# A fused attention block on 8 cores: a later and shared buffer for the first Q weights, and a thinner, later filler between the attention matmuls

## The chip, the cores and the metric

The kernel runs on the 8 cores of one Trainium2 chip, each core with one batch element and no traffic between cores. The metric is the device time of one execution in microseconds, which is that of the slowest core. Below, TensorE is called PE, VectorE DVE, ScalarE ACT, GpSimd POOL and SyncE SP, as in the profile.

## What is computed

Per core, x is 2048 x 1024 in f16; there are 16 heads of 64.

```python
xn = _layernorm(x, axis=-1)
q = shape_heads((xn @ wq.T + bq) * scaling);  k = shape_heads(xn @ wk.T + bk);  v = shape_heads(xn @ wv.T + bv)
scores = jnp.einsum('bhtd,bhsd->bhts', q, k)            # causal mask added
attn = jax.nn.softmax(scores.astype(jnp.float32) + mask, axis=-1).astype(jnp.float16)
out = jnp.einsum('bhts,bhsd->bhtd', attn, v)
s = out.transpose(0, 2, 1, 3).reshape(B, T, E) @ wo.T + bo
g = _silu(xn @ weight.T + pooled(xn) @ disha)
x = x + s * g
```

## The kernel before

The program is written by hand as five streams, one for each engine (`S.emit(queue, function, waits, semaphore)`), and each engine executes its stream strictly in the order in which the Python loops emitted it. Nothing reorders it later, so where a line stands in a loop decides what it is queued behind. SP issues nearly all loads, and a wait in its stream holds back every load behind it.

**Stage 1, lines 168 to 316.** For 16 tiles of 128 rows, `a_load` (L201) brings x into one of eight buffers `xin` on SP, `a_stats` and `a_sqrt_f` make mean and 1/std on DVE with a square root on ACT, `a_apply_f` (L234) normalises on DVE, `a_transp` (L242) transposes on PE, and `a_copy` (L251) moves the result to `xnT` on ACT. The loop `for t in range(NTT + 3)` emits statistics of tile t, the normalisation of tile t-1, and the transpose of tile t-2. In it stand, on SP, loads of the feed-forward weights into `wbig` (`mk_wT`, L264), the first half of the Q weights (`emit_wdma(0)` at t == 2, into a buffer `qsb` of its own) and, at t == 12, two loads into `D2`, whose memory is that of `xin0` and `xin1`. After the loop DVE makes eight tiles of `Weff` (L270) from `wbig` and `D2`.

**Stage 2, lines 318 to 413.** Q, K, V and gate products, each a group of 8 matmuls of 512 columns into one PSUM bank: L352 for Q and K, L380 for V, L404 for the gate with its SiLU on ACT (L410). Weights come in halves of 1 MB into `wsb0` and `wsb1`; `emit_wdma(idx)` for idx 0 to 5 names the half, and each waits until the matmuls that read the buffer before are done. `wsb0` shares memory with `xin2` and `xin3`, so whatever is loaded into it has to wait for `a_apply[11]`, the normalisation of tile 11.

**Stage 3, lines 426 to 722.** Attention proceeds by four blocks of 512 queries (tc 0 to 3), in each by 8 pairs of heads (p), in each by 4, 8, 12 or 16 key tiles (sc). One (tc, p, sc) is called a unit; there are 320, numbered u. A unit has two score matmuls (L659, L663, one for each head of the pair, 64 rows each, of N columns: 512, or 512, 384, 256 and 128 in the last four units of a pair, at the diagonal), an exponential on ACT over both (L672), in diagonal units a mask on POOL (L681), and two value matmuls (L698, L702), here called PV, which are emitted about five units later from the list `pvq`. The scores of unit u need the exponential of unit u-2, since two PSUM pairs alternate. After the last PV of a pair, `d_epilogue` copies the two accumulators out on DVE (L585, L587), and the first PV of the next pair waits for that; four small DMAs on SP follow. After the eighth pair the row sums of the block are in `L16`, and two units later DVE takes their reciprocal (L621).

**The filler.** Normalisation and output projection of a finished block are put between the attention matmuls of the next block. `fillq` has for each block 8 N tiles (one matmul L472 each, whose result multiplies `AttnOT` on DVE, L481; the first needs the reciprocal) and 8 E tiles (eight matmuls L515 with `woT` and one L520 with the bias; DVE multiplies and adds, POOL sends the output). `pop_chunk()` emits one N tile, or the next two matmuls of an E tile, so a block has 8 + 8 x 5 = 48 chunks. Each unit adds to `FS["credit"]`, up to `CCAP`, and chunks are popped while the credit is at least `CHUNK` = 440. The core of the loop in the order before:

```python
                    if len(pvq) >= 5:
                        pvq.pop(0)()
                    while FS["credit"] >= CHUNK:
                        ...
                    S.emit("tensor", ...)          # scores of unit u, then its exponential
                    pvq.append(pv_e)
                    FS["credit"] = min(CCAP, FS["credit"] + (300.0 + 2 * N) / 1.2 - 3 * N / 2.4)
```

What is left in `pvq` and `fillq` after the last unit, which includes all 48 chunks of the fourth block, is emitted at the end.

Of the kernel before, what the change touches and what calls it, by code (L numbers as in the profile page):

```python
# [7 lines left out]
F16 = mybir.dt.float16  # L8
# [4 lines left out]
NP = 128  # L13
# [31 lines left out]
def build_program(debug=False):  # L45
# [62 lines left out]
    qsb = at("qsb", [NP, ECH, 512], F16, o_KT + 4096)  # L108
# [42 lines left out]
    with ExitStack() as ctx:  # L151
# [122 lines left out]
        def emit_wdma(idx):  # L274
            src3 = wsrc[idx].rearrange("(ec p) o -> p ec o", p=NP)
            half = idx % 2
            dst = wsb[idx % 2]
            if idx == 0:
                ww = []
                dst = qsb  # L280
            elif idx == 1:
                ww = [("sPE", p_tp[NTT - 1])]
            elif idx == 2:
                ww = [("sPE", p_wdone[0]), ("sDVE", a_apply[11])]
            else:
                ww = [("sPE", p_wdone[idx - 2])]
            c_w[idx] = dma("sync", dst[:], src3[:, :, half * 512:(half + 1) * 512],
                           waits=ww, sem=f"sW{idx % 2}")

        for t in range(NTT + 3):  # L290
# [13 lines left out]
            if t == 2:  # L304
                emit_wdma(0)
            if t == 12:
                dma("sync", D2[0:64, :], disha_d,
                    waits=[("sDVE", a_apply[9])], sem="sD2")
                c_d2b[0] = dma("sync", D2[64:128, :], disha_d, sem="sD2")

# [28 lines left out]
        for pi, (widx0, bias, scale) in enumerate([(0, bqcs, s125), (2, bkcs, None)]):  # L339
            dst = QT if pi == 0 else KT  # L340
            for half in range(2):
# [3 lines left out]
                for tc4 in range(4):  # L345
                    for ocl in range(4):
                        oc = half * 4 + ocl
                        mms = []
                        wt_src = qsb if widx == 0 else wsb[wpar]
                        for ec in range(ECH):  # L350
                            mms.append(lambda g, ps, first, last, w=wt_src, ec_=ec, o_=ocl, t_=tc4:
                                       g.matmul(ps, w[:, ec_, o_ * NP:(o_ + 1) * NP],  # L352
# [6 lines left out]
                        if pi == 1 and half == 0:  # L359
                            ew.append(("sDVE", v_weff[ECH - 1]))  # L360
                            ew.append(("sPE", p_wdone[0]))
# [87 lines left out]
        CCAP = 1500.0  # L449
# [179 lines left out]
        for tc in range(NTC):  # L629
# [5 lines left out]
            for p in range(NPAIR):  # L635
                for sc in range(nsc):
# [4 lines left out]
                    if len(pvq) >= 5:  # L641
                        pvq.pop(0)()
                    while FS["credit"] >= CHUNK:
                        if not pop_chunk():
                            break
                        FS["credit"] -= CHUNK
# [39 lines left out]
                    def mk_pv(p_=p, tb_=tb, sl_=slot, o=off, n=N, a_exp_=a_exp, v_tri_=v_tri,  # L686
                              vv_=v_vevac[sc], s_=sc,
                              first=(sc == 0), last=(sc == nsc - 1)):
                        def go():
# [17 lines left out]
                            if last:  # L707
                                d_epilogue(p_, tb_, pv)
                        return go
                    pv_e = mk_pv()  # L710
                    pvq.append(pv_e)
                    u += 1
                    FS["credit"] = min(CCAP, FS["credit"]
                                       + (300.0 + 2 * N) / 1.2 - 3 * N / 2.4)
# [103 lines left out]
```

How the kernel before makes its waits and increments, by code:

```python
def build_program(debug=False):  # L45
# [669 lines left out]
        while pvq:  # L715
            pvq.pop(0)()
            while lnq:
                lnq.pop(0)[1]()
        while fillq or FS["cur"] is not None:
            assert pop_chunk(), "filler not ready at drain"
        flush_pend()
        flush_pend()
        for i2 in range(2):
            S.emit("gpsimd", lambda g, i_=i2: g.wait_ge(sems[f"sO{i_}"], last_out[i_]))
        if debug:
            dma("sync", dbg["dbg_AOT"], AttnOT[:],
                waits=[("sDVE", tc_norm[3][0]), ("sSH0", sh_last[0])], sem="sDBG")
            gw = [(s, max((v for s2, v in g_done.values() if s2 == s), default=None))
                  for s in ("sACT", "sDVE")]
            dma("sync", dbg["dbg_g"], g_sb[:], waits=gw, sem="sDBG")
            S.emit("sync", lambda g: g.wait_ge(sems["sDBG"], S.cnt["sDBG"]))
        globals()["_last_cnt"] = dict(S.cnt)
        def run(eng, q):
            lastw = {}
            for fn, waits, inc, amt, _val in S.ops[q]:
                for (s, v) in waits:
                    if lastw.get(s, -1) >= v:
                        continue
                    eng.wait_ge(sems[s], v)
                    lastw[s] = v
                inst = fn(eng)
                if inc is not None:
                    inst.then_inc(sems[inc], amt)
```

## Time and profile before

| | us |
|---|---|
| median of 2 runs | 789.04 (788.67 to 789.41) |
| the profiled execution | 790.79 |
| span of its slowest core, core 7, first to last instruction | 789.3 |
| spans of the other cores | 778.7 to 788.7 |
| core 7, mean granted TensorE clock | 0.890 |
| PE busy, ACT busy, DVE busy on core 7 | 653.7, 343.6, 251.5 |

The median is the number that a comparison is made with. The profiled execution took 1.75 us more than the median, 1.5 us of it outside the span of core 7. Busy time of PE includes overlapping matmuls and the half clock, so it is no measure of PE at its peak. A granted clock of 1.00 is 2.4 GHz and 0.50 is 1.2 GHz; a figure between them is a mean over a stretch that had both.

### The profile page before, as it was taken

To read this page: it belongs to the slowest core of one execution; us is meant where nothing else is said; L and a number is where in the kernel's file an instruction comes from. 1 tells how busy PE (TensorE), PEld (TensorE's weight loads), DVE (VectorE), ACT (ScalarE), POOL (GpSimd) and SP (SyncE) were. 2 spreads that over 40 slices of the span, in tenths; PEclk is the share of its full clock that TensorE was granted. 3 is DMA by queue.
4 is the path that set the end of the run, shared out by engine and by line. 5 is a ranking of instruction groups with operands and counts; after the bars stand their busy time and mean duration, and the time that the engine had idled before them with its cause. 6 is when DMAs were issued, how large, how long until landed. Compare 5 with 4: busy or idle time off the path is not lost.

```text
span 789.3 us, 8786 instructions; the slowest of 8 cores (778.7 to 789.3 us)
## 1 busy us (share of the span) xinstructions
PE 653.7 (83%) x2784; PEld 238.5 (30%) x2784; DVE 251.5 (32%) x372; ACT 343.6 (44%) x387; POOL 103.4 (13%) x164
## 2 busy tenths in 40 slices
PE   0457999999999997776888869988769999888665
PEld 0344444444333443221222212322211332222111
DVE  4886544443333000223233242231113222000154
ACT  0322000000000434553567746788864778888500
POOL 0000000000000001441133301321210122121101
PEclk9999999999999999555699967998975999999869
DMA  6424111011000001200211120110010111000022
GB/s 198 140 69 126 36 53 54 1 54 54 0 1 1 0 1 44 84 22 14 61 53 42 55 60 8 51 57 28 9 45 21 35 47 47 8 7 8 14 66 94
DMA packets 25696, 34.86 MB, mean 44 GB/s; under 512 B 4898, under 2 KB 19362, under 8 KB 25652
## 3 DMA queue, kind: packets, MB, share of 16 engines
q1 hardware_dynamic: 23092, 25.91, 11.5%
q0 software_dynamic: 2560, 8.39, 2.8%
q8 instruction: 24, 0.39, 0.2%
q14 instruction: 20, 0.16, 0.1%
HBM read 21.63 MB, written 8.39 MB: 38 GB/s over the span
## 4 chain that ended last, share of the span: by engine, by line
PE 68%; DVE 15%; issue 5%; DMA 4%; ACT 4%; SPq 2%; DVEq 1%; POOL 0%; ACTq 0%; POOLq 0%
PE PS L352 13%; PE PS L698 12%; PE PS L659 11%; PE PS L702 8%; PE PS L380 7%; PE PS L404 7%; PE Q L515 6%; ACT PT L672 4%; DVE OddB L587 3%; DVE OddA L585 3%; DVE L L621 2%; PE Q L472 2%; DMA xin<-x 1%; DVE xn L234 1%; PE PS L383 1%
## 5 line engine op out<-in xcount | busy, mean ns | idle before, releaser
L672 ACT ACTIVATE PT<-PS,neg 128x1024 f16<-128x1024 f32 (+1 forms) x320 | 302.7, 988 | 128.3 <-PE PS L663 125.7
L681 POOL TENSOR_TENSOR PT<-PT,tri 128x256 f16<-128x256 f16 x128 | 86.0, 682 | 611.9 <-ACT PT L672 610.1
L698 PE MATMUL PS<-PT,Vp 128*65 128x512 f16 (+1 forms) x320 | 134.2, 419 | 37.2 <-DVE OddB L587 36.9
L659 PE MATMUL PS<-QT,KT 64*128 64x512 f16 (+1 forms) x320 | 126.1, 395 | 14.1 <-ACT PT L672 10.9
L702 PE MATMUL PS<-PT,Vp 128*65 128x512 f16 (+1 forms) x320 | 127.7, 399 | 0.0
L663 PE MATMUL PS<-QT,KT 64*128 64x512 f16 (+1 forms) x320 | 127.2, 398 | 0.0
L585 DVE CAST OddA<-PS 65x512 f16<-65x512 f32 x32 | 22.0, 687 | 271.4 <-PE PS L702 258.9
L352 PE MATMUL PS<-xnT,wsb 128*128 128x512 f16 x384 | 83.0, 379 | 0.0
L410 ACT ACT_TABLE_LOAD x1 | 1.3, 1283 | 183.2 <-PE PS L404 183.2
L515 PE MATMUL Q<-woT,AttnOT 128*128 128x512 f16 x256 | 76.9, 400 | 4.1 <-DVE AttnOT L481 3.9
L659 PEld LDWEIGHTS PS<-QT,KT 64*128 64x128 f16 x320 | 30.1, 94 | 152.4 <-issue 152.4
L698 PEld LDWEIGHTS PS<-PT,Vp 128*65 128x65 f16 x320 | 36.4, 114 | 114.0 <-issue 108.9
L242 PE MATMUL PS<-eye,xn 128*128 128x128 f32 x128 | 31.0, 424 | 40.9 <-ACT xnT L251 26.6
L380 PE MATMUL PS<-wsb,xnT 128*128 128x512 f16 x256 | 60.8, 380 | 0.0
L404 PE MATMUL PS<-Weff,xnT 128*128 128x512 f16 x256 | 55.4, 379 | 0.0
L352 PEld LDWEIGHTS PS<-xnT,wsb 128*128 128x128 f16 x384 | 37.6, 98 | 45.3
L530 DVE TENSOR_TENSOR esb<-Q,g 128x512 f32<-128x512 f32 x32 | 22.1, 691 | 86.1 <-PE Q L520 47.7
L472 PE MATMUL Q<-L,hsel 16*128 16x512 f16 x32 | 18.1, 598 | 29.4 <-DVE L L621 25.7
L702 PEld LDWEIGHTS PS<-PT,Vp 128*65 128x65 f16 x320 | 39.4, 123 | 0.2
L242 PEld LDWEIGHTS PS<-eye,xn 128*128 128x128 f32 x128 | 25.1, 224 | 46.4 <-issue 46.4
L392 DVE CAST Vp<-PS 128x512 f16<-128x512 f32 x32 | 22.2, 694 | 46.4 <-PE PS L383 46.4
L515 PEld LDWEIGHTS Q<-woT,AttnOT 128*128 128x128 f16 x256 | 24.8, 101 | 31.8 <-issue 12.0
(41 smaller groups left out, 398.4 us busy)
## 6 DMA issues: line engine op xcount, KB each, us to landing
out<-esb POOLq DMA_DIRECT2D x32, 256.0 KB, 2.4
xin<-x SPq DMA_DIRECT2D x16, 256.0 KB, 5.0
wbig<-wT SPq DMA_DIRECT2D x8, 512.0 KB, 7.4
QT<-x SPq DMA_DIRECT2D x32, 128.0 KB, 2.4
wsb<-wkT SPq DMA_DIRECT2D x2, 1024.0 KB, 5.6
wsb<-wvT SPq DMA_DIRECT2D x2, 1024.0 KB, 5.4
woT<-woT SPq DMA_DIRECT2D x1, 2048.0 KB, 9.7
AttnOT<-OddA SPq DMA_DIRECT2D x32, 64.0 KB, 1.9
```

Of the source, the lines that this page charges most:

```text
L242: p_tp[tt] = S.emit("tensor", lambda g, jj=j, p=tt % 2: g.transpose(PS6[:, 4 + jj // 4, (jj % 4) * NP:(jj % 4 + 1) * NP], xn_sb[p][:, jj * ...
L352: g.matmul(ps, w[:, ec_, o_ * NP:(o_ + 1) * NP], xnT[:, ec_, t_ * 512:(t_ + 1) * 512], start=first, stop=last))
L380: g.matmul(ps, xnT[:, ec_, t_ * NP:(t_ + 1) * NP], wsb[w][:, ec_, :], start=first, stop=last))
L404: g.matmul(ps, xnT[:, ec_, t_ * NP:(t_ + 1) * NP], Weff[:, ec_, h * 512:(h + 1) * 512], start=first, stop=last))
L515: S.emit("tensor", lambda g: g.matmul(psF[sl], AttnOT[:, pc_, t_ * NP:(t_ + 1) * NP], woT[:, pc_, o * 512:(o + 1) * 512], start=first, sto ...
L585: evA = S.emit("vector", lambda g: g.tensor_copy(OddA[0:65, :], PS6[0:65, 4, :]), waits=wr, inc="sDVE")
L659: g.matmul(PS6[:, 2 * par_ + 0, o:o + n], KT[0:64, p_, sb2:sb2 + NP], QT[0:64, p_, t + o:t + 512], start=True, stop=True),
L663: g.matmul(PS6[:, 2 * par_ + 1, o:o + n], KT[64:128, p_, sb2:sb2 + NP], QT[64:128, p_, t + o:t + 512], start=True, stop=True),
L672: g.activation(PT[sl_][:, :, o:o + n], PS6[:, 2 * par_:2 * par_ + 2, o:o + n], AF.Exp, bias=neg2[:]), waits=we, inc="sACT")
L681: g.tensor_tensor(PT[sl_][:, :, o:o + NP], PT[sl_][:, :, o:o + NP], t, ALU.mult),
L698: S.emit("tensor", lambda g: g.matmul(psO(0, 65, 0, o, o + n), Vp[:, s_, (2 * p_) * 65:(2 * p_) * 65 + 65], PT[sl_][:, 0, o:o + n], start= ...
L702: pv = S.emit("tensor", lambda g: g.matmul(psO(0, 65, 1, o, o + n), Vp[:, s_, (2 * p_ + 1) * 65:(2 * p_ + 1) * 65 + 65], PT[sl_][:, 1, o:o ...
```

## The change

The change has three parts. `qsb` goes: the first half of the Q weights is loaded into `wsb0`, at t == 12 behind the `D2` loads, with a wait for the normalisation of tile 11; the waits that protected `qsb` go too. In the attention loop the scores of unit u are emitted first, then PV of the oldest unit, then the filler. And the credit for a unit is (172 + 2N)/1.2 - 3N/2.4 in place of (300 + 2N)/1.2 - 3N/2.4, with a cap of 2600 in place of 1500. For N = 512 the credit falls from 463.3 to 356.7, against 440 for a chunk.

```diff
@@ emit_wdma, and where it is called @@
-            dst = wsb[idx % 2]
             if idx == 0:
-                ww = []
-                dst = qsb
+                ww = [("sDVE", a_apply[11])]
             elif idx == 1:
                 ww = [("sPE", p_tp[NTT - 1])]
-            elif idx == 2:
-                ww = [("sPE", p_wdone[0]), ("sDVE", a_apply[11])]
             else:
                 ww = [("sPE", p_wdone[idx - 2])]
...
-            if t == 2:
-                emit_wdma(0)
             if t == 12:
                 dma("sync", D2[0:64, :], disha_d,
                     waits=[("sDVE", a_apply[9])], sem="sD2")
                 c_d2b[0] = dma("sync", D2[64:128, :], disha_d, sem="sD2")
+                emit_wdma(0)
@@ the waits of the projections @@
-                        if pi == 1 and half == 0:
-                            ew.append(("sDVE", v_weff[ECH - 1]))
-                            ew.append(("sPE", p_wdone[0]))
@@ the attention loop @@
-        CCAP = 1500.0
+        CCAP = 2600.0
...
-                    if len(pvq) >= 5:
-                        pvq.pop(0)()
-                    while FS["credit"] >= CHUNK:
-                        if not pop_chunk():
-                            break
-                        FS["credit"] -= CHUNK
                     par = u % 2
...
                     pv_e = mk_pv()
+                    if len(pvq) >= 5:
+                        pvq.pop(0)()
                     pvq.append(pv_e)
                     u += 1
                     FS["credit"] = min(CCAP, FS["credit"]
-                                       + (300.0 + 2 * N) / 1.2 - 3 * N / 2.4)
+                                       + (172.0 + 2 * N) / 1.2 - 3 * N / 2.4)
+                    while FS["credit"] >= CHUNK:
+                        if not pop_chunk():
+                            break
+                        FS["credit"] -= CHUNK
```

The SP stream in the second half of stage 1, before (`xin5` to `xin7` are the loads of tiles 13 to 15; `wsb1` gets the second half of the Q weights):

```order
L166 DMA xin3_67<-x 128x1024
L166 DMA xin4_68<-x 128x1024
L166 DMA D2_72<-disha 64x1024 x2
L166 DMA xin5_69<-x 128x1024
L166 DMA xin6_70<-x 128x1024
L166 DMA xin7_71<-x 128x1024
L166 DMA hsel_109<-hsel 16x1024
L264 DMA wbig_73<-wT 128x1024 x4
L166 DMA wsb1_54<-wqT 128x8x512
```

And the same place of the changed program:

```order
L165 DMA xin3_67<-x 128x1024
L165 DMA xin4_68<-x 128x1024
L165 DMA D2_72<-disha 64x1024 x2
L165 DMA wsb0_53<-wqT 128x8x512
L165 DMA xin5_69<-x 128x1024
L165 DMA xin6_70<-x 128x1024
L165 DMA xin7_71<-x 128x1024
L165 DMA hsel_108<-hsel 16x1024
L263 DMA wbig_73<-wT 128x1024 x4
L165 DMA wsb1_54<-wqT 128x8x512
```

The 1 MB load of Q weights now stands ahead of the x loads of tiles 13 to 15, with its wait for tile 11.

The PE stream in the second block (tc 1) at the first N tiles, before; `PT_63` is unit 31, the last of block 0:

```order
L698 MATMUL PS<-PT_63,Vp 65x128
L702 MATMUL PS<-PT_63,Vp 65x128
L659 MATMUL PS<-QT,KT 128x512
L663 MATMUL PS<-QT,KT 128x512
L698 MATMUL PS<-PT_111,Vp 65x512
L702 MATMUL PS<-PT_111,Vp 65x512
L659 MATMUL PS<-QT,KT 128x384
L663 MATMUL PS<-QT,KT 128x384
L698 MATMUL PS<-PT_112,Vp 65x512
L702 MATMUL PS<-PT_112,Vp 65x512
L472 MATMUL Q<-L_57,hsel 128x512 x3
L659 MATMUL PS<-QT,KT 128x256
```

And in the changed program (the names of `PT` have moved by one number):

```order
L682 MATMUL PS<-PT_63,Vp 65x128
L686 MATMUL PS<-PT_63,Vp 65x128
L643 MATMUL PS<-QT,KT 128x384
L647 MATMUL PS<-QT,KT 128x384
L682 MATMUL PS<-PT_110,Vp 65x512
L686 MATMUL PS<-PT_110,Vp 65x512
L643 MATMUL PS<-QT,KT 128x256
L647 MATMUL PS<-QT,KT 128x256
L682 MATMUL PS<-PT_111,Vp 65x512
L686 MATMUL PS<-PT_111,Vp 65x512
L462 MATMUL Q<-L_57,hsel 128x512 x5
L643 MATMUL PS<-QT,KT 128x128
```

Two scores and two PVs stand between the last PV of the block and the first N tile in both. The scores are one unit further on now, and five N tiles follow one another in place of three.

The PE stream at the end of the fifth pair of block 1, before: the chunk behind the PV of 384 columns, then the last two PVs of the pair, of 256 and 128 columns, each with its chunk:

```order
L515 MATMUL Q<-woT,AttnOT 128x512 x2
L659 MATMUL PS<-QT,KT 128x512
L663 MATMUL PS<-QT,KT 128x512
L698 MATMUL PS<-PT_60,Vp 65x256
L702 MATMUL PS<-PT_60,Vp 65x256
L520 MATMUL Q<-bo_sb,ones_77 128x512
L659 MATMUL PS<-QT,KT 128x512
L663 MATMUL PS<-QT,KT 128x512
L698 MATMUL PS<-PT_61,Vp 65x128
L702 MATMUL PS<-PT_61,Vp 65x128
L515 MATMUL Q<-woT,AttnOT 128x512 x2
```

And in the changed program, from the PV of 384 columns on:

```order
L682 MATMUL PS<-PT_112,Vp 65x384
L686 MATMUL PS<-PT_112,Vp 65x384
L643 MATMUL PS<-QT,KT 128x512
L647 MATMUL PS<-QT,KT 128x512
L682 MATMUL PS<-PT_60,Vp 65x256
L686 MATMUL PS<-PT_60,Vp 65x256
L505 MATMUL Q<-woT,AttnOT 128x512 x2
L643 MATMUL PS<-QT,KT 128x512
L647 MATMUL PS<-QT,KT 128x512
L682 MATMUL PS<-PT_61,Vp 65x128
L686 MATMUL PS<-PT_61,Vp 65x128
L510 MATMUL Q<-bo_sb,ones_76 128x512
```

Behind the PV of 384 columns stand scores now, and no chunk.

## Rows read from the trace of the kernel before

**Rows 1.** Page, granted clock in tenths, 40 equal slices, core 7

```profile
PEclk9999999999999999555699967998975999999869
```

**Rows 2.** Timeline, tiles 1 and 3 of stage 1: start us, duration us, engine, line, what

```profile
7.13 0.43 SPq L166 DMA_DIRECT2D qsb<-wqT  x1
...
18.82 0.69 DVE L209 BATCH_NORM_STATS2 st<-xin 128x6 f32<-128x512 f16 x1 [1.02 <-DMA xin<-x]
```

**Rows 3.** Timeline, the D2 loads, loads of tiles 13 to 15, tiles 11 and 13

```profile
46.12 1.19 SPq L166 DMA_DIRECT2D D<-disha  x2
...
47.37 1.51 SPq L166 DMA_DIRECT2D xin<-x  x3
...
52.07 0.81 DVE L234 TENSOR_SCALAR xn<-xin,mv,rstd 128x1024 f32<-128x1024 f16 x1
...
52.98 0.69 DVE L209 BATCH_NORM_STATS2 st<-xin 128x6 f32<-128x512 f16 x1
```

**Rows 4.** Page part 6, DMA issues: KB each, median us from issue to landing

```profile
xin<-x SPq DMA_DIRECT2D x16, 256.0 KB, 5.0
...
wsb<-wkT SPq DMA_DIRECT2D x2, 1024.0 KB, 5.6
...
wsb<-wqT SPq DMA_DIRECT2D x1, 1024.0 KB, 9.8
```

**Rows 5.** The tile xin, all its loads

```profile
DMA to landing us min/median/max: 2.5/5.0/12.2
```

**Rows 6.** Windows: us, busy PE, PEld, DVE, ACT, POOL, granted clock, DMA share, GB/s

```profile
50.00:52.00 2.00, 1.83 (x8) 1.43 (x8) 1.54 (x5) 0.00 (x0) 0.00 (x0) 1.00 0.92 250
```

**Rows 7.** The chain that ended last, from stage 1 into stage 2

```profile
66.65 1.24 DVE Weff L270
...
81.81 103.76 PE PS L352 x480
```

**Rows 8.** Timeline of PE in block 3 among E chunks

```profile
623.70 0.39 PE L659 MATMUL PS<-QT,KT 64*128 64x512 f16 x1
...
625.00 0.39 PE L659 MATMUL PS<-QT,KT 64*128 64x512 f16 x1
```

**Rows 9.** Timeline of PE in block 3 without filler

```profile
679.01 0.38 PE L698 MATMUL PS<-PT,Vp 128*65 128x512 f16 x1 [1.16 <-DVE OddB L587]
...
679.54 0.49 PE L659 MATMUL PS<-QT,KT 64*128 64x512 f16 x1
...
683.61 0.39 PE L659 MATMUL PS<-QT,KT 64*128 64x512 f16 x1
...
686.47 0.37 PE L659 MATMUL PS<-QT,KT 64*128 64x512 f16 x1
...
687.48 0.37 PE L659 MATMUL PS<-QT,KT 64*128 64x512 f16 x1
...
691.00 0.39 PE L659 MATMUL PS<-QT,KT 64*128 64x512 f16 x1
...
691.87 0.39 PE L659 MATMUL PS<-QT,KT 64*128 64x512 f16 x1
```

**Rows 10.** Windows: block 1 past its filler, block 3 without filler

```profile
434.00:444.50 10.50, 9.00 (x48) 2.92 (x47) 3.28 (x5) 8.32 (x10) 3.96 (x6) 1.00 0.21 71
...
666.10:679.60 13.50, 11.34 (x56) 3.38 (x54) 1.37 (x2) 12.82 (x14) 2.58 (x4) 1.00 0.00 0
679.70:683.10 3.40, 3.40 (x11) 0.66 (x10) 0.00 (x0) 2.23 (x2) 0.00 (x0) 0.50 0.16 39
```

**Rows 11.** Timeline of PE and DVE in block 1 at the first N tiles

```profile
368.30 1.01 PE L472 MATMUL Q<-L,hsel 16*128 16x512 f16 x2 [5.57 <-DVE L L621]
369.12 2.27 DVE L481 TENSOR_TENSOR AttnOT<-AttnOT,Q 128x512 f16<-128x512 f16 x3 [1.08 <-PE Q L472]
...
375.07 0.60 PE L472 MATMUL Q<-L,hsel 16*128 16x512 f16 x1
375.61 0.60 PE L659 MATMUL PS<-QT,KT 64*128 64x512 f16 x1
```

More of the change, by code:

```diff
@@ L107, in build_program @@
     wbig = at("wbig", [NP, 4, E], F32, o_KT + 16384)
-    qsb = at("qsb", [NP, ECH, 512], F16, o_KT + 4096)
     mo = o_misc
@@ L276, in emit_wdma @@
             half = idx % 2
-            dst = wsb[idx % 2]
             if idx == 0:
-                ww = []
-                dst = qsb
+                ww = [("sDVE", a_apply[11])]
             elif idx == 1:
                 ww = [("sPE", p_tp[NTT - 1])]
-            elif idx == 2:
-                ww = [("sPE", p_wdone[0]), ("sDVE", a_apply[11])]
             else:
                 ww = [("sPE", p_wdone[idx - 2])]
-            c_w[idx] = dma("sync", dst[:], src3[:, :, half * 512:(half + 1) * 512],
+            c_w[idx] = dma("sync", wsb[idx % 2][:], src3[:, :, half * 512:(half + 1) * 512],
                            waits=ww, sem=f"sW{idx % 2}")
@@ L348, in build_program @@
                         mms = []
-                        wt_src = qsb if widx == 0 else wsb[wpar]
                         for ec in range(ECH):
-                            mms.append(lambda g, ps, first, last, w=wt_src, ec_=ec, o_=ocl, t_=tc4:
-                                       g.matmul(ps, w[:, ec_, o_ * NP:(o_ + 1) * NP],
+                            mms.append(lambda g, ps, first, last, w=wpar, ec_=ec, o_=ocl, t_=tc4:
+                                       g.matmul(ps, wsb[w][:, ec_, o_ * NP:(o_ + 1) * NP],
                                                 xnT[:, ec_, t_ * 512:(t_ + 1) * 512],
```

## The prediction

> **What bounds the kernel now.** I read the page first for its clock line, then the chain that ended last, then the timeline of each place that the diff touches. The chain goes through DVE in stage 1: the normalisations, then `Weff` from 66.65 us on, and from 81.81 us PE alone, 480 matmuls of L352 in 103.76 us or 216 ns each [rows 7]. So stage 1 is bound by DVE, the projections by PE, and a delay of DVE in stage 1 goes to the end undiminished, since PE's first evacuation in stage 2 stands behind `Weff` on DVE. The clock line is at 9 throughout the projections, and at 5 to 8 in many slices from slice 16 on, which is attention [rows 1].
>
> Attention has two regimes at the full clock, read from the distance between the scores of successive units. Among E chunks PE sets the pace: 623.70 to 625.00 is 1.30 us for scores, two PVs and two L515 [rows 8]. Without filler ACT does: 686.47 to 687.48 is 1.01 us, one exponential of 1024 columns. Right behind a stall or the short diagonal units, when ACT has fallen behind or has had little to do, PE runs free at 691.00 to 691.87, 0.87 us [rows 9]. So a chunk costs PE 1.30 - 0.87 = 0.43 us, but added to a unit that waits for ACT it costs only 0.29.
>
> Once for each pair of heads PE waits for the copies of the accumulators, 1.16 us at 679.01 [rows 9]. In block 3 without filler the clock then falls: 679.70 to 683.10 is at 0.50, behind 13.5 us at 1.00 [rows 10]. The three units from 679.54 to 683.61 take 4.07 us [rows 9] where 0.87 + 0.87 + 1.01 = 2.75 would do, so one such fall costs 1.3 us there. Among chunks, where PE never waits for ACT, 3.4 us at half the clock do 1.7 us of work, so a fall costs up to 1.7.
>
> **Part 1, the Q weights.** What is removed: the 1 MB load at 7.13 us, ahead of the x load of tile 3. The statistics of tile 3 wait 1.02 us for that load [rows 2], and 1 MB takes about 4 us at the 250 GB/s of [rows 6], so without it the tile is there in time: -1.0 us, since DVE is the chain. Later loads in this part never keep DVE waiting, so nothing more is gained.
>
> What is added: SP waits for the normalisation of tile 11, which ends at 52.07 + 0.81 = 52.88, and then issues the 1 MB load and only after it the x loads of tiles 13, 14 and 15. Before, these were issued at 47.37, right behind the D2 loads [rows 3], and were there when the statistics of tile 13 started at 52.98. Queued behind SP's wait are also `hsel` and the four `wbig` loads; they were issued behind `Weff` anyway and shift with it. DVE waits from 52.98 until tile 13 lands, and everything on DVE behind it waits too: the normalisation of tile 12, the transposes, `Weff`, the first Q evacuation. A 1 MB load lands 5.6 us after its issue when it is alone, 9.8 when `wbig` loads stand ahead of it [rows 4]. Here it is nearly alone, the D2 loads of 6.8 us earlier being done, so 5.6. The 256 KB of tile 13 behind it add 1.0 us at 250 GB/s [rows 6]. That makes 52.9 + 5.6 + 1.0 = 59.5 against 52.98: **+6.5 us**. The bound below is the shortest landing of an x load, 2.5 us [rows 5], if its pieces overtook the weights; the bound above is 9.8 + 1.0 - 0.1 = 10.7. I take 6.5, because the row of a lone 1 MB load is nearest. Tiles 14 and 15 land 1 us apart, and one tile takes DVE at least 0.81 + 2 x 0.69 = 2.2 us [rows 3], so they cost nothing.
>
> The medians alone [rows 4] don't say whether one load may overtake another on SP's queue. The Trainium skill, page "DMA: Bandwidth & Descriptors", section "Queues, rings and completion order", says that an engine consumes descriptors in ring order, though completion is not strictly first in, first out. By that rule the term is near 6.5; if the loads shared the bandwidth freely it would be nearer 2.5. The 12.2 us that the slowest x load took [rows 5] agrees with the rule, as that load can only have waited for bytes ahead of it.
>
> The waits removed from the K projection cost nothing and give nothing: `Weff` and the first Q half are long done there. Sum of part 1: -1.0 + 6.5 = **+5.5 us**.
>
> **Part 2, the order in a unit.** Before, PE has PV, filler, scores; now scores, PV, filler. In a loop both are the same cycle. What changes is that PV runs one unit later against its scores. PE's wait for copies stands between the last PV of a pair and the first of the next, and the same chunk and the same scores stand between them as before; the order of the first N tiles shows it, two scores and two PVs in both. The seven `PT` buffers still suffice: the exponential of unit u needs PV of unit u-7, which stands ahead of the scores of u on PE. 0 us.
>
> **Part 3, rate and cap of the filler.** All 48 chunks of a block remain, so only their place matters. In the order of the programs the units behind a block's last chunk, by PV, number 15, 48 and 81 in blocks 1, 2 and 3 before, and 3, 35 and 71 now: 35 chunks move from among the others into what was bare. Each saves 0.43 us where it leaves and costs 0.29 where it comes to a unit that waits for ACT, and 0.43 where PE was catching up. By [rows 9] the bare pairs have about half their units of each kind, so 35 x 0.14 x 0.45 = **-2.2 us**.
>
> The cap lets five N tiles run together in blocks 1 and 3 and four in block 2, in place of three. The first waits for the reciprocal as before. The further ones go at DVE's pace, 2.27/3 = 0.76 us each, and before they stood between attention work for 375.61 - 375.07 = 0.54 each [rows 11]. Five N tiles moved by 0.22 are **+1.1 us**.
>
> The clock is the open term. Before, every pair among chunks except one (block 3's third) has a chunk behind each of its last three PVs, and the clock stays at 1.00 there; even past the filler of block 1 it still holds in 434.00 to 444.50 [rows 10]. Now 11 pairs among chunks lack one of the three, such as the fifth of block 1. No row shows what the clock does then. The bounds are no fall in 11, as in block 1, and a fall in each, as in bare block 3 [rows 10]. I take 3 falls of 1.6 us, +4.8, since the places are nearer to the full pattern than to the bare one. Against that, 2 or 3 bare pairs become covered, -2.5 x 1.3 = -3.3. Together **+1.5 us**, with bounds -3.3 and 11 x 1.6 - 3.3 = +14.3.
>
> **Sum.** 5.5 + 0 - 2.2 + 1.1 + 1.5 = +5.9 us on the profiled execution's 790.79, so 796.7; the median stood 1.75 us below that execution, so **795 us**. It is 0.8% slower, where about 2% (15.8 us) is what a measurement of this kernel tells from no change.
>
> **Rivals.** *A, the x load overtakes.* Tile 13 lands after 2.5 us, the part costs 1.5, the time is 791. For it: three loads were issued within 1.51 us and shared the queue. Against: the 9.8 us of a load with others ahead.
>
> *B, an even filler is a gain.* The thin pairs hold the clock, the covered ones no longer fall (-3.3), and catching up is worth 0.14 on all 35 moved chunks (-4.9): attention gives -7.1, the time is 795 - 0.4 - 7.1 = 788. For it: PE waits for nothing among chunks, and the clock in [rows 10] held past the filler of block 1. Against: half the bare units have no slack to give.
>
> *C, the thin pairs lose the clock.* The 11 pairs fall once each, at the copies' wait, and the time is 795 + 8 x 1.6 = 808, slower. It decides from about the ninth fall on: 795 + 6 x 1.6 = 804.6 with nine. For it: in bare pairs 1.16 us of waiting sufficed. Against: a chunk or two still stands at each place, and at half the clock PE is full, so the clock comes back.
>
> *D, the new rate does not spread the filler.* The order of the program excludes it.
>
> **Chances.** My forecast, 791 to 800: 0.50. A 0.12, B 0.20, C 0.12, and 0.06 for something else, of either sign. The range of 786 to 806 takes in B, the upper bound of the load term (799) and most of the way to C. Within 2% is up to 804.8: 0.86; slower 0.11; faster 0.03, for which no mechanism that I see is large enough.
>
> **What would show it.** In the profile after: the statistics of tile 13 wait for an x load by 6 to 7 us, that of tile 3 by nothing; the first of L352 stands 5.5 us later and the projections last the same; the scores of the last unit stand 6 us later; between full units among chunks distances of 1.30 and 0.87 alternate; and the clock among chunks shows a few short falls, in the stretches at 1.00 now. The prediction is wrong if x loads are not held behind the weights, or if half the clock holds for longer stretches than one pair.

## The result, and the profile after

The changed kernel takes 793.36 us (median of 11 executions, 791.8 to 794.87) against 789.47 for the kernel before on the same chip. The ratio is **1.0056, 95% interval 1.0042 to 1.0070**: slower, but by 0.56%, well inside 2%. The profiled execution took 792.77 us, and its slowest core is core 2. Executions in which one die ran at a lower clock are left out of all times and ratios below, while some of the expectations quote medians with such executions in them (785.2, 767.6 and 17.6 for what is 784.9, 767.4 and 17.5 here).

The page's clock line, and the span and mean granted clock of the slowest core, which answer to [rows 1]:

```profile
PEclk9999999999999999555698975999995999989969
```

```profile
core 2: 791.2 us, clock 0.894
```

In stage 1 the statistics of tile 13 now wait. Timeline of core 2, which answers to [rows 3] (start, duration, what, and in brackets the idle time before and what ended it):

```profile
51.59 0.81 DVE L233 TENSOR_SCALAR xn<-xin,mv,rstd 128x1024 f32<-128x1024 f16 x1
52.47 0.39 SPq L165 DMA_DIRECT2D wsb<-wqT  x1
52.91 2.89 SPq L165 DMA_DIRECT2D xin<-x  x3
...
60.78 0.69 DVE L208 BATCH_NORM_STATS2 st<-xin 128x6 f32<-128x512 f16 x1 [8.38 <-DMA xin<-x]
```

The bytes of that stretch, in its windows (us, busy PE, PEld, DVE, ACT, POOL, granted clock, DMA share, GB/s; the answer to [rows 6]):

```profile
54.00:55.00 1.00, 0.76 (x4) 0.36 (x2) 0.00 (x0) 0.00 (x0) 0.00 (x0) 1.00 0.09 14
55.00:56.00 1.00, 0.00 (x0) 0.00 (x0) 0.00 (x0) 0.00 (x0) 0.00 (x0) 1.00 0.60 176
56.00:57.00 1.00, 0.00 (x0) 0.00 (x0) 0.00 (x0) 0.00 (x0) 0.00 (x0) 1.00 1.17 293
57.00:58.00 1.00, 0.00 (x0) 0.00 (x0) 0.00 (x0) 0.00 (x0) 0.00 (x0) 1.00 0.91 317
58.00:59.00 1.00, 0.00 (x0) 0.00 (x0) 0.00 (x0) 0.00 (x0) 0.00 (x0) 1.00 0.69 174
59.00:60.00 1.00, 0.00 (x0) 0.00 (x0) 0.00 (x0) 0.00 (x0) 0.00 (x0) 1.00 1.00 369
```

The wait is 8.38 us, not 6.5. Until 55 us next to nothing moves, 2.5 us behind the issue. From issue to landing the weights and the three x loads behind them take, on the same core:

```profile
DMA to landing us min/median/max: 7.5/7.5/7.5
```

```profile
DMA to landing us min/median/max: 7.7/7.8/7.9
```

So the weights land at 59.98, and the three tiles behind them in their order, at 60.62, 61.30 and 61.92: tile 13 takes 0.64 us behind the weights, and the weights themselves take 7.5 where 5.6 was forecast. It is the same over the eight cores: the weights land 5.35 to 8.45 us behind their issue, median 7.4, tile 13 0.64 to 1.66 behind them, median 0.85, and the wait is 6.83 to 9.33 us, median 8.55. The chain that ended last goes through it, and then as in [rows 7]:

```profile
52.91 7.71 DMA xin<-x
...
88.58 103.76 PE PS L345 x480
```

The 480 matmuls last 103.76 us again, and they stand 6.8 us later than on the slowest core before. Later the shift shrinks: the scores of the last unit stand 4.2 us later in the median over cores (739.97 against 735.74), and 0.4 us later between the two slowest cores, not 6.

Now the sum by stretches, cut at the first and last scores of the attention; medians over eight cores, and the slowest core of each execution:

| us | before, median | after, median | before, core 7 | after, core 2 |
|---|---|---|---|---|
| start to first scores | 309.2 | 317.2 | 310.5 | 317.2 |
| block 0 | 42.2 | 42.7 | 42.5 | 42.7 |
| blocks 1 to 3, to the last scores | 385.0 | 380.6 | 389.4 | 382.9 |
| of these at half clock | 108.1 | 99.9 | 115.1 | 106.8 |
| last scores to the end | 46.7 | 47.5 | 46.8 | 48.4 |
| span | 782.3 | 787.4 | 789.3 | 791.2 |

So 8.0 us are lost ahead of the attention, and 4.4 come back in blocks 1 to 3, 6.5 on the cores that set the time. The clock goes with it. Before the change the cores differ in it by chance: core 2 had 95.8 us at half clock and took 379.6 for blocks 1 to 3, cores 0 and 7 had 115.1 and took 389.4. That is 9.8 us for 19.3, or **0.51 us for each microsecond at half clock**. Among the cores of the changed kernel it is less: core 7 has 92.0 us at half clock and takes 378.7, core 2 has 106.8 and takes 382.9, which is 0.29. Between the medians the half clock fell by 8.2 us. By the two slopes that is worth 2.4 to 4.2 us, an estimate, so most of the 4.4 us is clock and 0.2 to 2.0 the rest.

Where the clock fell, windows of core 7 after (columns as above; the answer to [rows 10]). First a stretch among chunks at the full clock, then the fall behind the fifth pair of block 1, those behind the fourth pair of block 2 and the second of block 3, and a stretch without a fall:

```profile
421.00:431.60 10.60, 8.46 (x42) 2.88 (x42) 3.48 (x6) 7.97 (x10) 4.12 (x6) 1.00 0.12 38
431.80:435.10 3.30, 3.30 (x10) 0.84 (x10) 1.33 (x2) 0.69 (x1) 1.34 (x3) 0.50 0.38 120
534.20:537.40 3.20, 3.20 (x10) 0.75 (x7) 0.98 (x2) 1.15 (x2) 0.00 (x0) 0.50 0.17 42
640.00:643.20 3.20, 3.20 (x9) 0.75 (x7) 0.90 (x2) 1.11 (x1) 0.54 (x1) 0.50 0.35 111
643.40:694.00 50.60, 45.95 (x219) 14.36 (x218) 8.97 (x13) 44.70 (x46) 10.45 (x16) 1.00 0.08 27
```

The first of these falls in the timeline of PE:

```profile
428.14 0.39 PE L643 MATMUL PS<-QT,KT 64*128 64x512 f16 x1
...
428.70 0.59 PE L505 MATMUL Q<-woT,AttnOT 128*128 128x512 f16 x2
...
429.78 0.38 PE L510 MATMUL Q<-bo_sb,ones 1*128 1x512 f16 x1
430.13 0.32 PE L643 MATMUL PS<-QT,KT 64*128 64x384 f16 x1
...
431.79 0.61 PE L682 MATMUL PS<-PT,Vp 128*65 128x512 f16 x1 [1.32 <-DVE OddB L577]
```

The two chunks of the pair's end are one of L505 and the bias matmul alone, then PE waits 1.32 us for the copies, and the clock falls. The falls behind block 2's fourth pair (534.2) and block 3's second (640.0) stand behind the same gap in the filler: of the last three PVs one has no chunk and one, the last, only the bias. The same three pairs fall on seven of the eight cores, where the other eight thin pairs hold. Two of those eight, block 1's seventh and block 2's third, also have one PV without a chunk and one with the bias alone, but not as the last.

The gap does not settle it, though. On core 2, the slowest, block 1's fifth pair holds, and the clock falls behind its third, fourth and sixth pair instead, of which the sixth has a chunk behind each of its last three PVs. The waits for the copies behind these pairs are the same on all cores. Behind the third pair it is 1.56 us, first on core 2 with the window that follows, then the same on core 7, where the clock stays at 1.00:

```profile
411.80 0.38 PE L682 MATMUL PS<-PT,Vp 128*65 128x512 f16 x1 [1.56 <-DVE OddB L577]
```

```profile
412.00:418.80 6.80, 6.80 (x19) 1.54 (x17) 1.74 (x2) 2.28 (x3) 2.31 (x4) 0.50 0.18 58
```

```profile
411.88 0.38 PE L682 MATMUL PS<-PT,Vp 128*65 128x512 f16 x1 [1.56 <-DVE OddB L577]
```

```profile
412.00:418.80 6.80, 6.80 (x34) 2.19 (x33) 1.68 (x2) 4.46 (x5) 2.38 (x4) 1.00 0.19 61
```

And two of the three places fell before the change too, though both pairs had a chunk behind each of their last three PVs, the bias behind the last. Block 2's fourth pair fell on seven cores, core 7 among them, behind a wait of 1.30 us; block 3's second fell on cores 1, 4 and 6. Windows of cores 7 and 1 before:

```profile
532.90:536.30 3.40, 3.40 (x11) 0.74 (x10) 0.69 (x1) 2.23 (x2) 0.54 (x1) 0.50 0.38 116
```

```profile
633.00:636.40 3.40, 3.39 (x9) 1.05 (x10) 1.35 (x2) 0.93 (x2) 0.54 (x1) 0.50 0.25 73
```

On core 7, apart from the starts of the blocks, the clock fell nine times before and six times after. Of the nine, seven stood behind bare pairs, one behind block 2's fourth pair and one behind block 3's third. Of the six, three stand behind bare pairs (575, 695 and 729 us).

In the distance between N tiles the cap did what was forecast. The N tiles of block 1, the answer to [rows 11]:

```profile
376.27 1.01 PE L462 MATMUL Q<-L,hsel 16*128 16x512 f16 x2 [4.83 <-DVE L L611]
377.10 3.87 DVE L471 TENSOR_TENSOR AttnOT<-AttnOT,Q 128x512 f16<-128x512 f16 x5 [1.08 <-PE Q L462]
378.72 0.58 PE L462 MATMUL Q<-L,hsel 16*128 16x512 f16 x1 [0.21 <-DVE AttnOT L471]
379.52 0.58 PE L462 MATMUL Q<-L,hsel 16*128 16x512 f16 x1 [0.22 <-DVE AttnOT L471]
```

They go 0.80 us apart, 3.87/5 = 0.77 of it DVE's, where 0.54 stood before.

### The profile page after: what moved, and what is told of

Read it like the earlier page. It is cut to its first block, busy times and chain, and to the rows that moved or that the text cites. A ratio compares the mean times of both kernels' runs of the same rounds, so it can differ in the third digit from the quotient of the medians.

```text
span 791.2 us, 8785 instructions; the slowest of 8 cores (784.5 to 791.2 us)
## 1 busy us (share of the span) xinstructions
PE 650.0 (82%) x2784; PEld 238.3 (30%) x2784; DVE 252.1 (32%) x372; ACT 341.5 (43%) x387; POOL 103.1 (13%) x164
## 4 chain that ended last, share of the span: by engine, by line
PE 69%; DVE 16%; issue 5%; DMA 4%; ACT 3%; SPq 1%; DVEq 1%; POOL 0%; ACTq 0%; POOLq 0%
PE PS L345 13%; PE PS L682 12%; PE PS L643 11%; PE PS L686 8%; PE PS L370 7%; PE PS L394 7%; PE Q L505 6%; ACT PT L656 3%; DVE OddB L577 3%; DVE OddA L575 3%; DVE L L611 2%; DVE xn L233 2%; DVE st L208 1%; DVE st L210 1%; DVE AttnOT L471 1%
## 5 line engine op out<-in xcount | busy, mean ns | idle before, releaser
L682 PE MATMUL PS<-PT,Vp 128*65 128x512 f16 (+1 forms) x320 | 131.9, 412 | 38.9 <-DVE OddB L577 38.9
L643 PE MATMUL PS<-QT,KT 64*128 64x512 f16 (+1 forms) x320 | 123.9, 388 | 12.8 <-ACT PT L656 9.9
L686 PE MATMUL PS<-PT,Vp 128*65 128x512 f16 (+1 forms) x320 | 126.4, 395 | 0.0
L647 PE MATMUL PS<-QT,KT 64*128 64x512 f16 (+1 forms) x320 | 125.1, 392 | 0.0
L345 PE MATMUL PS<-xnT,wsb 128*128 128x512 f16 x512 | 111.5, 381 | 1.3 <-DVE QT L355 1.3
L505 PE MATMUL Q<-woT,AttnOT 128*128 128x512 f16 x256 | 79.9, 412 | 2.2 <-DVE AttnOT L471 1.1
L345 PEld LDWEIGHTS PS<-xnT,wsb 128*128 128x128 f16 x512 | 50.3, 98 | 62.2 <-issue 2.6
L520 DVE TENSOR_TENSOR esb<-Q,g 128x512 f32<-128x512 f32 x32 | 22.1, 691 | 106.2 <-PE Q L510 72.6
L505 PEld LDWEIGHTS Q<-woT,AttnOT 128*128 128x128 f16 x256 | 25.4, 103 | 31.5 <-issue 12.1
```

The source lines that it names most:

```text
L345: g.matmul(ps, wsb[w][:, ec_, o_ * NP:(o_ + 1) * NP], xnT[:, ec_, t_ * 512:(t_ + 1) * 512], start=first, stop=last))
L505: S.emit("tensor", lambda g: g.matmul(psF[sl], AttnOT[:, pc_, t_ * NP:(t_ + 1) * NP], woT[:, pc_, o * 512:(o + 1) * 512], start=first, sto ...
L643: g.matmul(PS6[:, 2 * par_ + 0, o:o + n], KT[0:64, p_, sb2:sb2 + NP], QT[0:64, p_, t + o:t + 512], start=True, stop=True),
L647: g.matmul(PS6[:, 2 * par_ + 1, o:o + n], KT[64:128, p_, sb2:sb2 + NP], QT[64:128, p_, t + o:t + 512], start=True, stop=True),
L682: S.emit("tensor", lambda g: g.matmul(psO(0, 65, 0, o, o + n), Vp[:, s_, (2 * p_) * 65:(2 * p_) * 65 + 65], PT[sl_][:, 0, o:o + n], start= ...
L686: pv = S.emit("tensor", lambda g: g.matmul(psO(0, 65, 1, o, o + n), Vp[:, s_, (2 * p_ + 1) * 65:(2 * p_ + 1) * 65 + 65], PT[sl_][:, 1, o:o ...
```

## The experiments

### The parts alone

*Part 1 alone*, on the kernel before:

```diff
-                ww = []
-                dst = qsb
+                ww = [("sDVE", a_apply[11])]
...
-            if t == 2:
-                emit_wdma(0)
...
                 c_d2b[0] = dma("sync", D2[64:128, :], disha_d, sem="sD2")
+                emit_wdma(0)
```

> The kernel before with part 1 alone: no qsb, the first Q half goes to wsb0 behind the wait for tile 11 and ahead of the x loads of tiles 13 to 15. Theory (the whole cost of the change is DVE's wait for the x load of tile 13, the attention part is a gain): the statistics of tile 13 wait 6.5 to 8.5 us, stage 3 is as before, the time is 6 to 8 us over before. Rival (the change is slow in attention, and the shift of stage 1 is taken up later, for instance in a lucky phase of the clock): the time is within 3 us of before.

Measured 796.43 against 789.49, ratio 1.0103 (1.0076 to 1.0129): **+6.9 us**. The waits of its slowest core (in total, times, longest):

```profile
DVE st L208 <- DMA xin<-x: 10.3, 2, 9.2
```

*Parts 2 and 3 alone*, with the Q weights still in `qsb`:

```diff
-        CCAP = 1500.0
+        CCAP = 2600.0
...
                     pv_e = mk_pv()
+                    if len(pvq) >= 5:
+                        pvq.pop(0)()
...
-                                       + (300.0 + 2 * N) / 1.2 - 3 * N / 2.4)
+                                       + (172.0 + 2 * N) / 1.2 - 3 * N / 2.4)
+                    while FS["credit"] >= CHUNK: ...
```

> The kernel before with parts 2 and 3 alone: scores, PV, filler, with a credit of 172 and a cap of 2600; the Q weights are loaded early into qsb as before. Theory: attention is 3 to 6 us shorter, the time 3 to 6 us under before. Rival (the attention parts are worth nothing, as in the recorded sum): within 2 us of before. Second rival (the thin pairs lose the clock): 5 us or more over before.

Measured 785.73, ratio 0.9953 (0.9936 to 0.9971): **-3.8 us**. The two halves add up within their intervals: 6.9 - 3.8 = +3.1 against +3.9 for the whole. The load costs, the attention gives.

*The late Q weights behind the x loads*, in the changed kernel, still without `qsb`:

```diff
                 c_d2b[0] = dma("sync", D2[64:128, :], disha_d, sem="sD2")
-                emit_wdma(0)
+            if t == NTT - 1:
+                emit_wdma(0)
```

> The changed kernel with the first Q half issued behind the x loads of tiles 13 to 15 and ahead of hsel and the last four wbig loads; still no qsb. Theory (what costs is the place in SP's queue, not the late load itself): tile 13 waits for nothing, and the time is 6 to 8 us under the changed kernel, so 2 to 5 us under before. Rival (1 MB late in stage 1 costs wherever it stands, now by holding back wbig or by arriving late for the first Q matmul): at most 3 us under the changed kernel.

Measured 784.9, ratio 0.9947 (0.9927 to 0.9966): 8.4 us under the changed kernel and 4.6 under the one before. In its timeline the three x loads go out ahead and tile 13 waits for nothing:

```profile
46.35 1.53 SPq L165 DMA_DIRECT2D xin<-x  x3
...
51.95 0.39 SPq L165 DMA_DIRECT2D wsb<-wqT  x1
51.98 0.69 DVE L208 BATCH_NORM_STATS2 st<-xin 128x6 f32<-128x512 f16 x1
```

So the whole loss is the place of one `emit_wdma(0)` in SP's stream, not the shared buffer. The projections start 0.3 us earlier here than in the kernel with parts 2 and 3 alone (70.8 against 71.1, medians over cores), and that is all that taking the early load away is worth.

*Half of the bytes ahead*: the same weights as two loads of 512 KB, one ahead of the x loads and one behind:

```diff
-                emit_wdma(0)
+                dma("sync", wsb[0][:, 0:4, :], wq3[:, 0:4, 0:512],
+                    waits=[("sDVE", a_apply[11])], sem="sW0")
+            if t == NTT - 1:
+                c_w[0] = dma("sync", wsb[0][:, 4:8, :], wq3[:, 4:8, 0:512], sem="sW0")
```

> The changed kernel with the first Q half issued as two loads of 512 KB, one where the change puts it, ahead of the x loads of tiles 13 to 15, the other behind them. Theory (the x load of tile 13 lands behind the bytes ahead of it): DVE's wait for tile 13 falls from 8.4 us by the time of 512 KB, 2 to 3 us, to 5.5 to 6.5. Rival (the wait is mostly latency from issue to landing, whatever is ahead): it falls by less than 1 us. Second rival (the loads share the bandwidth in proportion, and the small one overtakes): it falls to 4 us or less.

It has too few executions to compare its time, so only its profile counts. The wait of tile 13 is 4.52 to 7.84 us over the cores, median 6.35 against 8.55. The slowest core's:

```profile
DVE st L208 <- DMA xin<-x: 9.0, 2, 7.4
```

Taking 512 KB away takes 2.2 us off, as much as they need at 240 GB/s. In the median over cores the half lands 5.0 us behind its issue, the whole 7.4, and tile 13 lands 0.9 us behind either. Half of the bytes thus still need two thirds of the time, so the wait is bytes only in part.

### The three edits of the attention, one at a time

*The order alone* (scores, PV, filler; rate 300 and cap 1500 kept):

```diff
-                    if len(pvq) >= 5:
-                        pvq.pop(0)()
-                    while FS["credit"] >= CHUNK: ...
...
                     pv_e = mk_pv()
+                    if len(pvq) >= 5:
+                        pvq.pop(0)()
...
+                    while FS["credit"] >= CHUNK: ...
```

> The kernel before with part 2 alone: scores, PV, filler in this order, credit 300 and cap 1500 as before. Theory (the order is the same cycle, only the rate of the filler matters): within 2 us of before. Rival (the order carries the gain of attention, since scores are one unit further on when PE waits for the reciprocal at the start of a block): 3 us or more under before.

Measured 794.12, ratio 1.0060 (1.0037 to 1.0083): **+4.6 us**, where I had put 0. Blocks 1 to 3 take 389.7 us (median) with 114.0 at half clock, against 385.0 with 108.1. By the slope of 0.51, 3.0 of these 4.7 us are clock. A second thing shows in its waits and in the timeline of its core 1: the first E tile now comes directly behind the last N tile, and PE waits for DVE to finish `AttnOT`.

```profile
PE Q L515 <- DVE AttnOT L481: 5.0, 3, 2.8
```

```profile
479.55 0.60 PE L472 MATMUL Q<-L,hsel 16*128 16x512 f16 x1
...
481.27 1.01 PE L515 MATMUL Q<-woT,AttnOT 128*128 128x512 f16 x2 [1.12 <-DVE AttnOT L481]
```

In the kernel before that wait was 3.9 us in all. The order is not free: with the same credits another unit gets each chunk, and which of the two effects weighs more I did not separate.

*The rate alone*, `(300.0 + 2 * N)` to `(172.0 + 2 * N)`, and *the cap alone*, `CCAP` 1500 to 2600, each on the kernel before:

> The kernel before with the credit of 172 alone, cap 1500, order as before. Theory after the order alone turned out 0.6% slower: the lower rate carries all of the gain of attention and more, because moved chunks pay less where they arrive than they save where they leave, and fewer bare pairs fall to half the clock; 4 to 9 us under before. Rival (rate and order only work together, since thin places then lie elsewhere): within 2 us of before.

> The kernel before with the cap of 2600 alone. Theory (five N tiles in a row cost DVE's pace, 0.22 us for each that runs on, but the first E tile comes one or two units earlier and ends the stretch at half the clock sooner): within 2 us of before. Rival (the burst is a cost, as in the recorded sum and somewhat more): 2 to 5 us over before. Second rival (the burst is what shortens the first pair of blocks 2 and 3 by 1 us each and the second by more): 2 to 4 us under before.

Rate alone 787.5 against 789.3, ratio 0.9979 (0.9967 to 0.9991): -1.8 us, where 4 to 9 were expected. Cap alone 786.12, ratio 0.9958 (0.9941 to 0.9974): -3.2 us, where at most 2 were expected. The half clock of blocks 1 to 3 moved the other way with the rate, 108.1 to 114.4, and fell to 95.7 with the cap. The single edits add up to -0.21 - 0.42 + 0.60 = -0.03%, and together they give -0.47%: **they are not additive**. The gap of 0.44% is not much more than the intervals allow (0.35% taken together). Each edit shifts every chunk, and with the chunks the places of the falls. Taking the clock out by the slope of 0.51 leaves, as an estimate from the medians of blocks 1 to 3 (385.3, 382.9 and 389.7 us against 385.0), -2.9 us for the rate, +4.3 for the cap and +1.7 for the order, which add up to +3.1, where the three together leave -0.2. That the rate alone saves anything with 6.3 us more at half clock speaks for the catching up of the units; it was not measured apart.

### Filling the wait that brings the clock down

Once per pair PE waits for the copies. If the wait is part of the cause, independent matmuls put exactly there should remove both the wait and the fall. Two chunks are forced ahead of the first PV of each pair and paid for by the credit, so the total is the same:

```diff
                     if len(pvq) >= 5:
-                        pvq.pop(0)()
-                    pvq.append(pv_e)
+                        if pvq[0][1]:
+                            for _ in range(2):
+                                if pop_chunk():
+                                    FS["credit"] -= CHUNK
+                        pvq.pop(0)[0]()
+                    pvq.append((pv_e, sc == 0))
```

On the kernel with the late load:

> The changed kernel with the late load behind the x loads, and with two chunks forced in ahead of the first PV of each pair, where PE waits for the copies of the accumulators (they are paid from the credit, which may go negative). Theory (PE's wait of 1.2 to 1.5 us for DVE's copies is idle time that filler can use, and chunks beside it keep the clock up): each of some 17 filled waits saves up to 0.8 us, so 6 to 13 us under the same kernel without the forced chunks, which measured 785.2. Rival (the scores of the next unit are held back by the forced chunks and ACT starves as long as PE gains): within 2 us of that kernel. Second rival (the units behind the wait are now bare and lose the clock): slower than that kernel.

Measured 767.4, ratio 0.9726 (0.9703 to 0.9748): **17.5 us** under the same kernel without it, more than the 6 to 13 expected. Its timeline in block 1 shows four L506, then a wait of 0.35 us where 1.32 stood:

```profile
419.32 0.32 PE L644 MATMUL PS<-QT,KT 64*128 64x384 f16 x1
...
419.59 1.04 PE L506 MATMUL Q<-woT,AttnOT 128*128 128x512 f16 x4
420.98 0.38 PE L683 MATMUL PS<-PT,Vp 128*65 128x512 f16 x1 [0.35 <-DVE OddB L578]
```

The waits on the copies, over the slowest core's whole execution; first the kernel with the late load, then this one:

```profile
PE PS L683 <- DVE OddB L578: 38.8, 31, 1.6
```

```profile
PE PS L683 <- DVE OddB L578: 25.7, 26, 1.5
```

In the medians over cores that is 12.5 us less waiting (39.4 to 26.9), and the half clock of blocks 1 to 3 goes from 98.1 to 88.2 us, worth 2.9 to 5.0 by the two slopes. Blocks 1 to 3 take 365.6 us in place of 380.2, so 14.6 less, and waiting and clock are enough for that. The rest shows between the slowest cores, whose blocks 1 to 3 take 384.2 us with 110.2 at half clock without the forced chunks, and 366.1 with 93.2 with them. The three thin pairs that fell in the changed kernel fall on no core now, behind waits of 0.35, 0.10 and 0.10 us. In the order of the two programs, what stands behind each PV of such a pair is (EE two matmuls of an E tile, e its bias matmul, - nothing):

```
                        changed kernel           with two forced chunks
block 1, fifth pair     e - EE EE EE - EE e      - - - EE EE - EE eEEEE
block 2, fourth pair    EE ... EE EE EE - e      - - ... EE EE EE - eEEEE
block 3, second pair    EE ... EE EE EE - e      - - ... EE EE EE - eEEEE
```

The last three places are the same, and only the copies' wait behind them has got its two chunks. So at these three pairs the filler and the wait for the copies bring the clock down only together. No run separates the shorter wait from the four matmuls of 128 rows that stand in it. What is left of falls are bare pairs at the end of blocks 2 and 3, where no chunk is left to force.

The same on the kernel before:

> The kernel before, with nothing of the change, and with two chunks forced in ahead of the first PV of each pair. Theory (the gain of the forced chunks comes from PE's wait for the copies and does not need the change): 9 to 14 us under before, somewhat less than the 17.6 us that they gave on top of the late load, since the filler here ends earlier and fewer pairs have it. Rival (they pay only together with the thinner filler, whose thin places they repair): at most 5 us under before.

Measured 778.3 against 789.66, ratio 0.9854 (0.9837 to 0.9871): -11.4 us. The half clock of blocks 1 to 3 hardly moves here (107.2 us for 108.1, medians), so the gain is the waiting. The slowest core waits 28.9 us for the copies, against 36.9 before.

Three chunks in place of two:

> As the kernel that measured 767.6 (late load behind the x loads, two forced chunks), but with three forced chunks. Theory (PE's wait of 1.2 to 1.6 us holds two chunks of 0.43 us and most of a third): within 2 us of 767.6, since what the third fills of the wait, it takes from the units behind. Rival (each further chunk is a gain as long as the pair's credit pays for it): 764 or less. Second rival (the third runs past the wait and holds back the scores): 770 or more.

Measured 764.2, ratio 0.9674 (0.9660 to 0.9689), 3.2 us better than two. The wait fell to 22.1 us in 18 places, in place of 25.7 in 26:

```profile
PE PS L683 <- DVE OddB L578: 22.1, 18, 1.6
```

The third chunk does cover what two left open at eight places; the first rival had it nearly.

With two forced chunks the others of blocks 2 and 3 are still spent before the block ends. A smaller credit there spreads them to the last pair:

```diff
-                                       + (172.0 + 2 * N) / 1.2 - 3 * N / 2.4)
+                                       + ((172.0 + 2 * N) / 1.2 - 3 * N / 2.4)
+                                       * (1.0, 1.0, 0.75, 0.5)[tc])
```

> As the kernel that measured 767.6, with the credit of a unit multiplied by 0.75 in block 2 and 0.5 in block 3, so that the filler reaches nearly to the end of each block. Theory (each pair that keeps two forced chunks saves its wait and one fall of the clock, together about 2 us, and six more pairs have them): 5 to 10 us under 767.6. Rival (with half of the units of a pair bare and PE waiting for ACT between them, the clock falls elsewhere, and N tiles drawn out over more units lengthen the stretch at half the clock at the start of a block): slower than 767.6.

Measured **757.75, ratio 0.9604 (0.9586 to 0.9621)**: 9.7 us under two forced chunks alone, 31.9 under the kernel before. Block 3 past its start, windows of core 6, its slowest: the clock is at 1.00 in all three, and PE and ACT are both busy over 90% of the time but for the last window's PE.

```profile
640.00:660.00 20.00, 19.30 (x93) 6.00 (x92) 4.15 (x6) 18.25 (x21) 5.58 (x9) 1.00 0.06 20
660.00:680.00 20.00, 19.23 (x93) 5.94 (x91) 2.76 (x4) 18.41 (x20) 4.79 (x8) 1.00 0.14 47
680.00:700.00 20.00, 17.96 (x87) 5.53 (x86) 4.96 (x8) 18.24 (x19) 3.11 (x5) 1.00 0.07 21
```

Seven of eight cores have no fall left in block 3 apart from its start, and the spans are 752.8 to 756.2, against 778.7 to 789.3 before: with the falls goes most of the difference between the cores.

The spread alone, without forced chunks:

> As the changed kernel with the late load behind the x loads (785.2), with the same spreading of the filler over blocks 2 and 3 and no forced chunks. It shows what thin filler does alone. Theory (a pair whose last three PVs lack a chunk loses the clock once more often than not when two are lacking; catching up is worth little): one fall for most pairs, 1 to 6 us over 785.2. Rival (even spreading is a gain by catching up, whatever the clock does): under 785.2.

Measured 780.5, ratio 0.9871 (0.9843 to 0.9899), 4.4 us under the kernel with the late load, where 1 to 6 over it were expected. Its executions differ more than the others' (774.85 to 782.6), so the size is rough. The waits for the copies stay, 39.3 us in all on its slowest core, in 31 places.

The short falls go down, from 23.9 to 10.2 us per core (median). So spreading alone takes short falls away and leaves the waits, and forcing removes the waits; together they give 27.2 us over the late load (784.9 to 757.75), more than 17.5 + 4.4.

## Why the prediction was right

The time, 793.4 for 795 forecast, and the sign are right. Step by step:

- **The wait for tile 13** is the mechanism named, in its place, and goes through the projections undiminished: part 1 alone costs 6.9 us, and moving the load behind the x loads gives 8.4 back. The term was mis-sized: +6.5 forecast, 8.55 measured (median over cores). In the step "5.6 + 1.0" the 1.0 for tile 13 is about right, 0.85 in the median. The 5.6 is too small, as the weights took 7.4 to land. It was the median of two lone loads on core 7; over all cores of the kernel before, the four lone loads of 1 MB took 5.0 to 8.1 us each. That is not all of it, and why most cores were slower here, where all issue the load between 52.0 and 52.5 us of their spans, stays open. Rival A, an overtaking at 1.5 us, is out. The Trainium skill, page "DMA: Bandwidth & Descriptors", section "Queues, rings and completion order", has descriptors consumed in ring order with completion not strictly so. The trace agrees with the first half, as on all eight cores tiles 13, 14 and 15 landed behind the weights and in their order; no run here shows a completion out of order. The 2.5 us before bytes moved on core 2 are not peculiar to the late load either: the late weights had moved their first 50 KB 1.3 to 2.9 us behind the issue, the lone loads before 1.3 to 2.7 us. Windows of core 7 before, from the issue of a lone load at 102.77:

```profile
102.77:103.77 1.00, 1.00 (x6) 0.47 (x5) 0.81 (x1) 0.00 (x0) 0.00 (x0) 1.00 0.00 0
103.77:104.77 1.00, 1.00 (x7) 0.47 (x5) 0.17 (x1) 0.00 (x0) 0.00 (x0) 1.00 0.72 111
```

- **The wait for tile 3**: -1.0 forecast, 0.3 measured. The 1.02 us of [rows 2] is core 7's, the longest; core 0 waited 0.85, cores 3, 5 and 1 0.49, 0.34 and 0.25, and the other three not at all. The wait is gone on all cores after the change. Part 1 up to the first scores is thus +8.0 for +5.5.
- **The order**: 0 forecast, +4.6 measured when made alone. The step "in a loop both are the same cycle" failed. The cycle is the same, but the chunks fall to other units. In the whole change it can't be told apart from rate and cap, which are not additive.
- **The moved chunks and the cap**: -2.2 + 1.1 = -1.1 forecast, and what blocks 1 to 3 gain beside the clock is 0.2 to 2.0 us by the two slopes. That bears out the sum of the two terms but not the terms: made alone, the rate leaves -2.9 beside the clock and the cap +4.3, both by the slope of 0.51. The distances are as forecast: among full units behind chunks 1.31 and without a chunk 0.87, and five N tiles 0.80 apart:

```profile
626.81 0.39 PE L643 MATMUL PS<-QT,KT 64*128 64x512 f16 x1
...
627.68 0.39 PE L643 MATMUL PS<-QT,KT 64*128 64x512 f16 x1
...
628.99 0.39 PE L643 MATMUL PS<-QT,KT 64*128 64x512 f16 x1
```

- **The clock**: "3 falls in 11 thin pairs" came out as three, partly by luck. The premise beside it, that before the change the clock stays at 1.00 among chunks, is wrong: it fell behind block 2's fourth pair on seven cores and behind block 3's second on three, and these are two of the three places. The other term, "2 or 3 bare pairs become covered", was too small. On core 7 five of the nine falls went: three behind bare pairs that got chunks, one behind block 3's third pair, whose end is full now, and one behind a pair that stayed bare. Against them stand two new ones, and block 3 starts with one stretch of 20.5 us at half clock in place of 23.9. The clock gave -2.4 to -4.2 us in blocks 1 to 3 (by the two slopes) where +1.5 stood in the sum. Rival C, each thin pair falling, is out: on seven cores eight of the eleven held. Rival B, an even filler as a gain, was right for the attention in sign and in half its size: -3.8 us with parts 2 and 3 alone, where it had -7.1.

So two terms were off in opposite directions, the load by about +2.5 and the attention by about -4 (3.8 under against +0.4), and the sum came out 1.6 us under the forecast. That the time came so near is partly the luck of that cancellation. The sign rests on the load, whose place and wait were understood and whose size was not.

## What to carry to other kernels

A load put into a queue's stream takes its wait and its bytes to everything behind it: before moving one, read who waits for the loads behind, since here one line further down was worth 8.4 us. Fill an unavoidable wait of PE with independent matmuls at that very place, rather than by an average rate; it removes most of the wait and, here, the falls of the clock behind it, 2.2% in all, and spreading the rest until the last pair gave 1.3% more. Where the clock falls at one pair on one core and not on another with the same program, small edits of an order move the time by half a per cent in either direction and don't add up, so judge them together, by the half clock of each core and not of the slowest alone.

## What the runs showed of the hardware

- Half clock costs 0.51 us per microsecond in blocks 1 to 3 of the kernel before (cores of one execution that do the same work: 379.6 us with 95.8 at half clock, 389.4 with 115.1), and 0.29 in the changed one (378.7 with 92.0, 382.9 with 106.8). Three cores of the kernel before, 0, 5 and 7, have the same 34.1 us of short falls each and are its three slowest.
- Falls to 1.2 GHz stood behind waits of 1.07 to 1.56 us, and the same wait at the same pair of the same program was followed by a fall on one core and by none on another (1.56 us behind block 1's third pair, cores 2 and 7). Neither the length of the wait nor the chunks of the pair's end alone decides it. With the waits filled to 0.35 and 0.10 us the pairs that fell on most cores held 2.4 GHz on all eight.
- Loads issued one behind the other on SP landed in that order on all eight cores. An x tile of 256 KB behind 1 MB landed 0.64 to 1.66 us behind it and made DVE wait for 6.83 to 9.33 us; the 1 MB, issued on every core between 52.0 and 52.5 us of its span, took 5.35 to 8.45 us to land.
